# Local attention with the values held in the array, two heads side by side, in a kernel of an SSM mixer and two transformer layers

## What is computed

```python
def _layer(x, wqkv, qs, ksc, wo, lg, lb, w1, b1, w2, b2):
    h = shift_token(x)
    q, k, v = split(h @ wqkv)               # 8 heads of 64
    q, k = rotary_xpos(l2norm(q) * qs, l2norm(k) * ksc)
    # windows of 128 tokens: each sees itself and the one before, masked
    sim = jnp.einsum('bhwid,bhwjd->bhwij', bq * 8, bk)
    attn = jax.nn.softmax(jnp.where(mask, -big, sim), axis=-1)
    out = jnp.einsum('bhwij,bhwjd->bhwid', attn, bv)
    x = x + out.reshape(b, n, 512) @ wo
    h = layernorm(shift_token(x)) * lg + lb
    a, g = jnp.split(h @ w1 + b1, 2, axis=-1)   # 682 each
    return x + (a * gelu(g)) @ w2 + b2
```

## Time and profile before

| what | value |
|---|---|
| median of 3 runs | 5043.82 us (5042.55 to 5043.82) |
| the profiled execution's own time | 5045.3 us |
| its span, first to last instruction | 5043.5 us |
| mean granted clock of PE | 0.969 of 2.4 GHz |
| PE busy over the span | 4616.9 us (92%) |
| DVE, ACT, POOL busy | 76%, 56%, 42% |

### The profile page before, as it was taken

How to read it: one execution, slowest core, us unless ns; L and a number is a source line. 1 busy time by engine, 2 the same in 40 slices (tenths; PEclk the granted TensorE clock), 3 DMA queues, 4 the chain that set the end, 5 groups by cost and what they waited for, 6 DMA issues and landing times. The chain is left out here.

```text
span 5043.5 us, 60534 instructions
## 1 busy us (share of the span) xinstructions
PE 4616.9 (92%) x19870; PEld 2872.0 (57%) x19870; DVE 3826.2 (76%) x6091; ACT 2821.1 (56%) x5904; POOL 2111.0 (42%) x932
## 2 busy tenths in 40 slices
...
PEclk7999999999999999599999999999999999999999
...
GB/s 69 101 109 115 112 113 106 112 115 113 113 121 109 111 104 92 126 9 26 13 17 22 13 26 14 17 22 38 58 18 22 30 17 30 22 22 30 18 26 22
DMA packets 112566, 299.36 MB, mean 59 GB/s; under 512 B 18940, under 2 KB 39008, under 8 KB 111488
## 3 DMA queue, kind: packets, MB, share of 16 engines
...
## 5 line engine op out<-in xcount | busy, mean ns | idle before, releaser
L1425 POOL TENSOR_TENSOR b_by_cos<-b_qk,b_rotary 128x1024 f32<-128x1024 f32 x128 | 319.4, 2495 | 2595.3 <-DVE b_qk L1460 2595.3
L840 POOL TENSOR_TENSOR a_state<-a_state,a_c_wide 128x1024 f32<-128x1024 f32 x512 | 1194.2, 2361 | 47.1 <-DVE a_state L780 45.9
L561 PE MATMUL a_y_sum<-a_state,a_ident 128*128 128x512 f32 x2048 | 971.5, 612 | 9.1 <-POOL a_state L840 9.1
L780 DVE TENSOR_TENSOR_SCAN a_state<-a_decay,a_slot 128x1024 f32<-128x1024 f32 x320 | 722.4, 2279 | 42.3 <-PE a_y_sum L561 30.5
L1191 PE MATMUL b_bank<-b_w_qkv,b_hx_part 128*128 128x512 f32 x2304 | 622.1, 413 | 92.0 <-DVE b_hx_part L1437 60.4
L561 PEld LDWEIGHTS a_y_sum<-a_state,a_ident 128*128 128x128 f32 x2048 | 399.8, 197 | 426.3 <-issue 374.8
L1302 PE MATMUL b_bank<-b_hn_part,b_w 128*128 128x512 f32 x2112 | 527.1, 400 | 67.6 <-ACT b_gelu L1406 61.2
L1360 ACT ACTIVATE b_scores<-b_scores,b_row_bias 128x256 f32<-128x256 f32 (+1 forms) x1024 | 477.8, 469 | 175.7 <-DVE b_row_bias L1506 175.2
L1191 PEld LDWEIGHTS b_bank<-b_w_qkv,b_hx_part 128*128 128x128 f32 x2304 | 425.7, 192 | 235.9 <-DVE b_hx_part L1437 62.0
L1302 PEld LDWEIGHTS b_bank<-b_hn_part,b_w 128*128 128x128 f32 x2112 | 385.5, 188 | 166.7 <-ACT b_gelu L1406 81.9
L833 POOL TENSOR_TENSOR a_state<-a_u,a_b_wide 128x1024 f32<-128x1024 f32 x192 | 450.9, 2362 | 59.0 <-PE a_y_sum L561 58.0
...
## 6 DMA issues: line engine op xcount, KB each, us to landing
a_c_wide<-bc_rows SPq DMA_DIRECT2D x256, 512.0 KB, 3.7
...
```

What stands on the lines that cost most here:

```text
L561: last = nc.tensor.matmul(y_sum[dd][:], ident[:], state[state_ring.slot[q]][:, i, :], start=False, stop=(j == GROUPS - 1 and i == GROUP - 1))
L780: nc.vector.tensor_tensor_scan(flat(h), flat(factor), flat(term), 0.0, ALU.mult, ALU.add).then_inc(scan_done.sem, 1)
L840: nc.gpsimd.tensor_tensor(h[:], h[:], c_wide[c_ring.slot[q // 2]][:], ALU.mult).then_inc(cmul_done.sem, 1)
```

## The change

- `att` has the operands the other way round. 64 columns of `v` are the weights and the 128 columns of `probs_t` move. The output has the features of a head on 64 partitions and the tokens along the row. An even head goes to partitions 0 to 63 and an odd one to 64 to 127, in turn. What comes out is already in the layout of `o_t`.
- `ot` and `otc` go. The row sums take their place: `rate` (DVE, the reciprocal alone), `rx` (POOL, writes the reciprocal of each head 64 times along the row to `rate_wide`), `rt` (PE, four transposes of `rate_wide`), `rtc` (ACT, copies them to `rate_t`). `onorm` (DVE) is then the output times `rate_t`, and writes `o_t`.
- `rate_wide` and `rate_t` have one buffer each, so `rx` waits for the `rtc` of the window before, and `rtc` for the `onorm` of the window before.
- The last block of `w_2` and of `h2` is filled up with zeros once, and `wd` takes 128 rows for it too.
- `ORDER` is another list.

```diff
-mask:0.0 exp:0 score:0.0 add:0 mask:0.1 hxs:0 add:1 mask:1.0 cen:0 mask:1.1 wo:0 score:0.1 psq:0 sq:0 wo:1 score:1.0
...
+exp:0 hxload:0 score:0.0 mask:0.0 mask:0.1 wo:0 score:0.1 add:0 hxs:0 wo:1 add:1 mask:1.0 score:1.0 x1load:0 rate:0
...
+                nc.vector.memset(w_2[:, HID_CHUNKS - 1, :], 0.0)
+                nc.vector.memset(h2[:, HID_CHUNKS - 1, :], 0.0)
+                nc.vector.memset(one[:], 1.0)
...
-                for h in range(HEADS):
-                    blocks = (0, 1) if w else (1,)
+                blocks = (0, 1) if w else (1,)
+                for p in range(PAIRS):
                     for blk in blocks:
-                        last = nc.tensor.matmul(psum.tile(f"o{w}")[:, h * DIM_HEAD:(h + 1) * DIM_HEAD], probs_t[w % 2][:, 2 * h + blk, :],
-                                                v[slot][:, w - 1 + blk, h * DIM_HEAD:(h + 1) * DIM_HEAD],
-                                                start=(blk == blocks[0]), stop=(blk == 1))
+                        for h in range(2):
+                            at = (2 * p + h) * DIM_HEAD
+                            last = nc.tensor.matmul(psum.tile(f"o{w}")[h * DIM_HEAD:(h + 1) * DIM_HEAD, p * WINDOW:(p + 1) * WINDOW],
+                                                    v[slot][:, w - 1 + blk, at:at + DIM_HEAD], probs_t[w % 2][:, 2 * (2 * p + h) + blk, :],
+                                                    start=(blk == blocks[0]), stop=(blk == 1))
...
-            def turn_output(s, slot, w):
...
+            def turn_rate(s, slot, w):
+
+                pe.wait_ge(rate_wide_done.sem, rate_wide_done.at(s, w + 1))
+                psum.wait_free(pe, s, f"r{w}")
                 for p in range(PAIRS):
...
+                    last = nc.tensor.transpose(psum.tile(f"r{w}")[:, p * WINDOW:(p + 1) * WINDOW],
+                                               rate_wide[:, 2 * p:2 * p + 2, :].rearrange("p h d -> p (h d)"), ident)
...
-                    last = nc.tensor.matmul(psum.tile(f"wd{m}")[:], w_2[0:hid_rows(k), k, m * P:(m + 1) * P],
-                                            h2[0:hid_rows(k), k, :], start=(k == 0), stop=(k == HID_CHUNKS - 1))
+                    last = nc.tensor.matmul(psum.tile(f"wd{m}")[:], w_2[:, k, m * P:(m + 1) * P], h2[:, k, :], start=(k == 0), stop=(k == HID_CHUNKS - 1))
...
+            def copy_rate(s, slot, w):
+                act.wait_ge(o_t_done.sem, o_t_done.at(s, w))
+                psum.wait_full(act, s, f"r{w}")
+                nc.scalar.activation(rate_t[:], psum.tile(f"r{w}")[:].rearrange("p (n c) -> p n c", c=WINDOW), ACT.Copy)\
+                    .then_inc(rate_t_done.sem, 1)
...
+            def widen_rate(s, slot, w):
+                pool.wait_ge(row_rate_done.sem, row_rate_done.at(s, w + 1))
+                pool.wait_ge(rate_t_done.sem, rate_t_done.at(s, w))
+                nc.gpsimd.tensor_tensor(rate_wide[:], row_rate[:, w, :].unsqueeze(2).to_broadcast([P, HEADS, DIM_HEAD]),
+                                        one[:].unsqueeze(2).to_broadcast([P, HEADS, DIM_HEAD]), ALU.mult)\
+                    .then_inc(rate_wide_done.sem, 1)
...
+            def normalise(s, slot, w):
+                dve.wait_ge(x2_done.sem, x2_done.at(s))
+                dve.wait_ge(rate_t_done.sem, rate_t_done.at(s, w + 1))
                 psum.wait_full(dve, s, f"o{w}")
...
+                nc.vector.tensor_tensor(o_t[:, :, w * WINDOW:(w + 1) * WINDOW],
+                                        psum.tile(f"o{w}")[:].rearrange("p (n c) -> p n c", c=WINDOW), rate_t[:], ALU.mult)\
+                    .then_inc(o_t_done.sem, 1)
```

More of the change, by code:

```diff
@@ L850 @@
 STEPS = {1: "hxload hxs pq pk psq pss prate pnorm prot padd ptr ptc v vc",
-         2: "resload score mask exp pt att onorm ot otc",
+         2: "resload score mask exp rate rx rt rtc pt att onorm",
          3: "wo add mean cen sq sqs var dev xn hn hns ga gelu gated wd fin store sum turn turnc x1load outstore"}
@@ L856 @@
 ORDER = """
-mask:0.0 exp:0 score:0.0 add:0 mask:0.1 hxs:0 add:1 mask:1.0 cen:0 mask:1.1 wo:0 score:0.1 psq:0 sq:0 wo:1 score:1.0
-pq:0 pss:0 hxload:0 sqs:0 mean:0 score:1.1 pnorm:0 pk:0 prate:0 pt:0.0 pt:0.1 score:2.0 exp:1 mask:2.0 resload:0
-prot:0 var:0 v:0 padd:0 pt:1.0 vc:0 onorm:0 att:0 score:2.1 ptc:0 dev:0 mask:2.1 pt:1.1 ptr:0 psq:1 pq:1 x1load:0 pk:1
-pt:1.2 pss:1 pt:1.3 prate:1 score:3.0 pnorm:1 ot:0 att:1 mask:3.0 prot:1 exp:2 padd:1 xn:0 otc:0 vc:1 v:1 ptc:1
-score:3.1 onorm:1 hns:0 hn:0 pt:2.0 outstore:0 ptr:1 mask:3.1 pq:2 pk:2 psq:2 pss:2 gated:0 pt:2.1 pt:2.2 ga:0 ga:1
-gated:1 gelu:0 prate:2 pnorm:2 pt:2.3 ot:1 prot:2 gelu:1 padd:2 gated:2 onorm:2 exp:3 vc:2 gelu:2 otc:1 ga:2 gated:3
-v:2 att:2 ga:3 gelu:3 store:0 gated:4 gelu:4 pt:3.0 ptc:2 ptr:2 pt:3.1 psq:3 ga:4 gelu:5 pss:3 gated:5 ga:5 prate:3
-fin:0 pq:3 pk:3 pt:3.2 wd:0 turnc:0 pt:3.3 pnorm:3 wd:1 prot:3 att:3 turnc:1 sum:0 turn:0 fin:1 turn:1 ot:2 ptr:3
-sum:1 padd:3 onorm:3 ptc:3 otc:2 otc:3 ot:3 v:3 vc:3
+exp:0 hxload:0 score:0.0 mask:0.0 mask:0.1 wo:0 score:0.1 add:0 hxs:0 wo:1 add:1 mask:1.0 score:1.0 x1load:0 rate:0
+psq:0 pq:0 mean:0 cen:0 resload:0 pk:0 pss:0 pt:0.0 rx:0 mask:1.1 score:1.1 rt:0 pnorm:0 pt:0.1 mask:2.0 prate:0
+score:2.0 sq:0 rtc:0 exp:1 att:0 outstore:0 prot:0 vc:0 v:0 rx:1 score:2.1 padd:0 pt:1.0 sqs:0 ptr:0 onorm:0 ptc:0
+var:0 dev:0 mask:2.1 pt:1.1 pq:1 xn:0 pk:1 psq:1 pt:1.2 score:3.0 pss:1 rate:1 pt:1.3 prate:1 store:0 v:1 exp:2 hn:0
+vc:1 pnorm:1 pt:2.0 mask:3.0 att:1 prot:1 score:3.1 padd:1 hns:0 ptr:1 rx:2 ptc:1 onorm:1 rt:1 rtc:1 mask:3.1 pss:2
+rate:2 pq:2 psq:2 pk:2 pt:2.1 prate:2 pnorm:2 pt:2.2 ga:0 exp:3 rtc:2 pt:2.3 rt:2 prot:2 padd:2 vc:2 rate:3 rx:3
+onorm:2 ptc:2 v:2 gated:0 pss:3 gated:1 gelu:0 att:2 pt:3.0 psq:3 gelu:1 prate:3 ptr:2 pt:3.1 pq:3 pk:3 gelu:2 pnorm:3
+gated:2 ga:1 gelu:3 gated:3 vc:3 ga:2 pt:3.2 gated:4 gated:5 v:3 gelu:4 ga:3 ga:4 ga:5 fin:0 prot:3 wd:0 wd:1 gelu:5
+padd:3 sum:0 fin:1 sum:1 pt:3.3 rt:3 ptr:3 turnc:0 turnc:1 turn:0 ptc:3 onorm:3 turn:1 att:3 rtc:3
 """
@@ L932, in stack_pass @@
         row_rate = sb("row_rate", [P, TILES, HEADS])
-        o = [sb(f"o{i}", [P, INNER]) for i in range(2)]
+        rate_t = sb("rate_t", [P, PAIRS, WINDOW])
+        rate_wide = sb("rate_wide", [P, HEADS, DIM_HEAD])
         o_t = sb("o_t", [P, PAIRS, SEQ])
```

38 lines of the change are left out of this document (13 added, 25 removed).

## The result

| | before | after |
|---|---|---|
| median | 5043.39 us (5042.55 to 5043.82, 4 runs) | 4896.28 us (4891.48 to 4898.66, 4 runs) |
| ratio | | 0.9707, 95% interval [0.969, 0.9724] |
| profiled execution | 5045.3 us | 4896.68 us |
| its span | 5043.5 us | 4894.9 us |

The change makes the kernel 2.9% faster; 3.0% was forecast, and the time lies inside the range.

A forecast was written before the change was run, and what follows sets the result against it. PE was taken as the bound: its work changes by -6.0 us a pass and waits by +1.0, so -5.0 over 31 passes, -155 us, takes 5045.3 to 4890 us. The 8-in-10 range was 4830 to 4970 us.

The forecast's parts named there:

- Attention itself: att on PE: two heads run at once in the column halves, 56 steps of 0.109 us, 12.6 to 6.1 us a pass.
- Switches: PE between whole and divided array, 0.17 to 0.2 us each: zeros in wd save 0.7 us a pass, att adds 1.2.
- PE's own work: PE's work without waits: 85.4 us of a pass, changing by -6.0 to about 79.4.
- The waits: PE's idle time: old waits of 4.7 us a pass go, new ones of 5.7 come, +1.0 us.
- The sum of the walk: Waits followed step by step through the new order, at score:2.0, att:0, v:1, wo:0, two ptr and the rest: 5.7 us.
- `rx`: New on POOL, four a pass at 1.2 us: nothing in the sum; might hold DVE up to 4.8 us a pass.
- The granted clock is 1.00, so nothing is to be won or lost there: PE's clock over a pass: taken to stay at its upper level, so no term for it in the sum.
- The waits do not grow: Rival on PE's waits: they stay at 2 to 4.7 us a pass, 4774 to 4858 us; chance 0.17.
- The waits eat the gain: Rival: the rate, rx, rt, rtc, onorm chain brings 8 to 10 us of waits a pass, 4960 to 5022 us; chance 0.17.
- The column halves take turns: Rival in att: 112 x 0.109 = 12.2 us, loads hidden, 5078 or 5044 us; chance 0.13 together with exposed loads.

The follow-up runs named there:

- Experiment 1: The changed kernel, with all products of a window's even heads run before those of its odd heads: 4979.85 us, ratio 0.9872 to the kernel before.
- experiment 2: The kernel before, with only the last block of w_2 and h2 zero-filled and multiplied over 128 rows in wd: 5021.21 us, ratio 0.9954.
- Experiment 5: The changed kernel, with the copy of pt:0.1 moved from DVE to ACT, behind prate:0: 4883.64 us, ratio 0.9679 to the kernel before.
- experiment 3: The changed kernel, with the step order of the kernel before and the new steps placed into it: 5074.65 us, ratio 1.0058 to the kernel before.
- numbers 9 and 10: var:0 put ahead of ptr:0 and sqs:0 ahead of the sine, on the kernel of Experiment 5 (4879.57 us) and on the changed kernel (4896.82 us).

## Why the prediction came out right

By its own steps:

- **Attention itself: right.** The step was taken as 0.109 us against an upper bound of 0.22. The visits sum to 3 x 1.90 + 1.02 = 6.7 us, switches included, where 6.1 for the steps and 1.2 for the switches were put. In the trace the two matmuls of a pair start 6 or 7 ns apart, and one pair follows the other at 0.109 us. Experiment 1 shows what this is worth: without it the visits take 3.3 us. The bound that I chose by the nearest row, the transposes with 128 moving columns, was the right one. The rule of the Trainium skill ("TensorE: Matmul & The Clock Gate", section "Part 3: Packing small matmuls — row/col tiling") that a weight load overlaps only with a matmul in other rows does not hold in this trace: the loads of both halves use the same 128 rows, take 0.14 us each and run while matmuls run, so that a matmul and its load together take 0.059 us of a visit.
- **Switches: right for `wd`, not shown apart for `att`.** The zeros were put at -0.7 us a pass, and experiment 2 measured -0.7 a pass and 22 to 24 us in all. The six switches of `att`, put at +1.2, have no run of their own; steps and switches together came out 0.6 us less than put.
- **PE's own work: right.** Forecast 79.4 us of a pass, measured 84.8 - 5.9 = 78.9.
- **The waits: right in place, nearly so in size, wrong in kind.** Forecast and measured: `score:2.0` 1.3 and 1.1; `att:0` 1.0 and 0.85; `v:1` 1.8 and 1.4; the two `ptr` 1.0 and 1.3; `wo:0` 0.3 and 0.2; the rest 0.3 and nothing. The sum of the walk was 5.7, and I had not added to it the overlap that each wait breaks off, though the 4.7 beside it holds them; measured are 4.9 without and 5.9 with them. I had also walked each wait as a price of its own. Experiment 5 shows that the one of `att:0` is not: without it, `ptr:0` waits instead. Had I put nothing at `att:0`, the pass would have come out the same. So the agreement of the terms says less about each of them than it seems to.
- **`rx`: right, for a reason that it did not have.** 1.2 us was estimated and 1.04 measured, at no cost. By the rule of the Trainium skill ("SBUF — State Buffer", section "SBUF: two separate sides") DVE might have been held up to 4.8 us a pass. Nothing of the kind is seen for `rx`, and this order does not put the rule to the test there: each DVE instruction with a tensor as input that ran beside an `rx` from 2300 to 4800 us has an input in PSUM (`pnorm`, the copies of `pt`, `onorm`, `cen`, two parts of `mask`), and none took more than about 0.01 us over its usual time. DVE is busy 58.9 us of a pass, against 61.3. For the cosine the rule agrees with the trace, where `sqs` goes from 0.69 to 1.68 us. Shortest, median and longest ns of the sine and of `rx` from 2300 to 4800 us, against the earlier trace rows:

```profile
L1487 DVE TENSOR_TENSOR b_qk_rot<-b_qk,b_rotary x232: 675/683/2419, 2303.9 to 4761.3; 128x512 f32<-128x512 f32 x116
...
L1440 POOL TENSOR_TENSOR b_rate_wide<-b_row_rate,b_one x117: 1038/1039/1041, 2315.5 to 4793.0; 128x512 f32<-128x512 f32 x117
```

- **"The granted clock is 1.00, so nothing is to be won or lost there": this step failed.** The change put two waits of 1.1 and 0.85 us within 3 us of each other, and in ten passes the clock falls at them, which costs 13 us. The error was hidden by another: the sum took 5.0 us from each of 31 passes, while the short passes gave 5.3 and 5.1 and the last two 8.5 and 6.0. That the total came within 7 us is therefore in part luck: the passes and the end gave 12 us more than the sum had, while the clock and a later first `var` took 18 that it did not have.
- **The rivals.** "The waits do not grow" did not happen. "The waits eat the gain" did not happen to after, but experiment 3 shows it real: it is what the change does in the order of before, and the chain from `rate` over `rx` to `rt`, which it names, is in the rows as a late `rx` ahead of `rt` (2.3 us a pass). The open table changes and the falls of the clock are there too, and it names neither. I had given it its chance for the new order and had not seen that the new order is what wards it off. "The column halves take turns" is what experiment 1 makes by hand, and it gave 4980 and not 5078: the visits take 11.3 us a pass, where 12.2 and 1.2 for the switches were put, and the pass takes up only 2.7 of the 4.5 us by which they grow against after.

The balance in us, of the spans: attention and zeros take 6.5 from PE's own work in each pass and the waits give 1.2 back. From the first `var` to the thirtieth that makes 138.2 less, the falls of the clock included; the last two passes give 14.5, the stretch behind them 1.0, and before the first `var` 5.2 are lost: 148.5 of the 148.6 measured.

What stays open: why the clock falls in some passes and not in others whose waits are equal to 0.01 us; how many falls exactly an execution without a profile has (its mean granted clock, 0.964 to 0.966 in the runs of after, speaks for about as many as the ten of the profiled one); what of the wait of `v:1` and the later windows would remain if `ptr:0` came earlier, since numbers 9 and 10 did not bring it earlier; and whether an order exists in which the chain of the windows is off PE's path.
